# Four cross-attention layers on one core: wide layers' K and V projected in front of the layers, Q once per layer, one key tile for all queries per step

## The reference

```python
def _L0_xattn_ref(hidden_states, encoder_hidden_states, mask_A, mask_B, Wq, Wk, Wv, Wo, bo, ...):
    q, k, v = hidden_states @ Wq, encoder_hidden_states @ Wk, encoder_hidden_states @ Wv   # 16 heads of 64
    logits = jnp.einsum('bhqd,bhkd->bhqk', q, k) * scale + col_bias   # bias in two pairs of key columns
    probs = jax.nn.softmax(logits, axis=-1)
    out = jnp.einsum('bhqk,bhkd->bhqd', probs, v)
    return out.transpose(0, 2, 1, 3).reshape(B, HW, 1024) @ Wo + bo + residual
```

## Time and profile before

| | |
|---|---|
| median of 3 timed runs | 5464.57 us (5464.24 to 5474.47) |
| span of the profiled execution, first to last instruction | 5460.9 us |
| instructions | 81,559 |
| mean granted TensorE clock | 0.969 |
| DMA traffic | 116.57 MB |

### The profile page before, as it was taken

The page is one execution under the profiler, slowest core; times in us unless marked ns, Lnnn a source line. Parts: engine busy times, 40 slices in busy tenths (PEclk is TensorE's granted clock), DMA queues, the critical chain, the costliest instruction groups (busy, mean ns, idle before and its releaser), DMA issues.

```text
span 5460.9 us, 81559 instructions
## 1 busy us (share of the span) xinstructions
PE 5173.7 (95%) x21484; PEld 2708.9 (50%) x21484; DVE 3684.8 (67%) x5908; ACT 2245.5 (41%) x4042; POOL 2695.0 (49%) x2048
## 2 busy tenths in 40 slices
PE   7999999999979898987999999999989999999999
PEld 4455545554444444444455555555445455545554
DVE  6767676767667676765767666676676667676767
ACT  2433344334425455552444444344424444444443
POOL 1656565656510101011656566666625656565655
PEclk8999999999979999997999999999989999999999
DMA  2010101010020101001010101010011010101010
GB/s 72 14 27 14 27 14 27 14 27 14 14 43 15 24 16 23 16 15 26 14 26 13 26 13 26 13 26 19 8 28 24 16 26 13 26 13 26 13 26 17
DMA packets 40356, 116.57 MB, mean 21 GB/s; under 512 B 7350, under 2 KB 20150, under 8 KB 35068
## 3 DMA queue, kind: packets, MB, share of 16 engines
q1 hardware_dynamic: 39938, 112.04, 9.4%
HBM read 26.86 MB, written 2.10 MB: 5 GB/s over the span
## 4 chain that ended last, share of the span: by engine, by line
PE 82%; issue 7%; DVE 6%; DMA 2%; SPq 1%; ACT 0%; DVEq 0%; POOL 0%; ACTq 0%; POOLq 0%
PE OB L654 19%; PE SS L594 13%; PE ST L625 11%; PE ST L627 9%; PE ST L551 5%; PE ST L567 4%; PE OB L786 4%; DVE mpart L1087 4%; PE ST L765 3%; PE SS L744 3%; PE ST L572 3%; PE ST L672 3%; PE ZB L607 2%; DMA Q<-rawQ 1%; PE ZB L744 1%
## 5 line engine op out<-in xcount | busy, mean ns | idle before, releaser
L282 POOL TENSOR_TENSOR acc<-acc,P 128x512 f32<-128x512 f32 (+1 forms) x1776 | 2362.5, 1356 | 455.1 <-ACT P L934 308.8
L934 ACT ACTIVATE P<-ST 128x512 f32<-128x512 f32 (+1 forms) x2496 | 1385.5, 597 | 2012.0 <-PE ST L627 1703.7
L1087 DVE TENSOR_REDUCE mpart<-SS 128x1 f32<-128x400 f32 (+1 forms) x3072 | 1665.0, 563 | 764.1 <-PE SS L594 709.1
L654 PE MATMUL OB<-P,V 128*64 128x512 f32 (+1 forms) x4992 | 1348.0, 618 | 1.1
L594 PE MATMUL SS<-KS,Q 128*128 128x400 f32 (+1 forms) x3072 | 1171.6, 387 | 70.2 <-DVE mpart L1087 67.1
L625 PE MATMUL ST<-Q,K 128*128 128x512 f32 (+1 forms) x2496 | 1061.3, 425 | 32.9 <-issue 18.3
L594 PEld LDWEIGHTS SS<-KS,Q 128*128 128x128 f32 x3072 | 585.0, 192 | 860.0 <-DVE mpart L1087 758.5
L627 PE MATMUL ST<-Q,K 128*128 128x512 f32 (+1 forms) x2496 | 989.6, 396 | 0.0
L278 POOL TENSOR_TENSOR acc<-P 128x512 f32<-128x512 f32 x192 | 241.3, 1278 | 1410.8 <-ACT P L934 1310.8
L625 PEld LDWEIGHTS ST<-Q,K 128*128 128x128 f32 (+1 forms) x2496 | 462.8, 185 | 515.8 <-ACT P L934 348.3
L1106 DVE RECIPROCAL R<-ZB 128x64 f32<-128x64 f32 (+1 forms) x432 | 371.3, 860 | 408.9 <-PE ZB L607 408.9
(11 more groups left out here) (126 smaller groups left out, 3608.1 us busy)
## 6 DMA issues: line engine op xcount, KB each, us to landing
Q<-Q SPq DMA_DIRECT2D x48, 512.0 KB, 4.5
KS<-K SPq DMA_DIRECT2D x48, 400.5 KB, 3.8
K<-K SPq DMA_DIRECT2D x48, 400.5 KB, 5.3
Q<-Q SPq DMA_DIRECT2D x32, 256.0 KB, 4.3
wk<-in_wk SPq DMA_DIRECT2D x25, 256.0 KB, 4.4
wv<-in_wv SPq DMA_DIRECT2D x25, 256.0 KB, 4.6
Q<-rawQ SPq DMA_DIRECT2D x16, 256.0 KB, 3.8
wq<-in_wq SPq DMA_DIRECT2D x25, 128.0 KB, 4.3
```

The lines of the kernel that those rows point to most:

```text
L282: eng.tensor_tensor(out, out, P[0:rows_of(t), u % NP, :], ALU.add).then_inc(done, raised)
L654: last = pe.matmul(OB[64 * jj:64 * jj + 64, :], V[0:k, t, 64 * b:64 * b + 64], P[0:k, (2 * s + jj) % NP, :], start=t == 0, stop=t == KT - 1)
L934: act.activation(P[0:k, u % NP, :], ST[u % 4][0:k, :], ACT.Exp, scale=SCALE).then_inc(act_p, 1)
L1087: dve.tensor_reduce(mpart[:, i // len(KCH), i % len(KCH):i % len(KCH) + 1], SS[i % 2][:, 0:w], AX.X, ALU.max).then_inc(dve_s, 1)
```

## The change

The program has no hardware loops any more. In front of all layers, ctx is split into high and low parts (`ch`, `cl`), and so are the weights; K (all 24 pairs, and the narrow layer's K and V) and V (six quads of four pairs) are projected with three fp32r matmuls (high x high, high x low, low x high) per 128 channels instead of one in fp32, and go to tensors in HBM (`dK`, `dV`). The split Wq goes to `dWq`. At the start of a wide layer, `q_phase` projects Q of all heads in 32 items of 128 channels x 512 queries and stores both parts in `dQ`; from item 10 on the maxima tiles of the first head run between the items. A head's keys, queries and values are loaded by SP up to three heads ahead. A step of `head` is one key tile for four chunks of 512 queries, with three score banks `ST`, two value banks `OA`, `OB`, and three banks `SS` that maxima tiles, the transposed maxima, the sums and the output share in a fixed order (`RING`). `P` holds four key tiles of 2048. DVE adds the exponentials of key tiles 1 and 2, POOL those of 3 to 12, in halves of 1024. The output of a pair stands among the scores of the next pair's second head, at key tiles 0 to 3. The sums of a head come behind key tile 2 of the next. Maxima tiles run up to two heads ahead at key tiles 11 and 12. The narrow layer keeps its order, without loops, with its K and V from the front and 16 instead of 9 tiles of exponentials.

```diff
-NP = 6
-STEPS = 2 * KT
+NP = 4
+DVE_T = (1, 2)
+POOL_T = range(3, KT)
+NSTG = 6
+def s_tiles(h, t):
+    if t >= KT - 2:
+        return 2, (part(SUNITS, t - KT + 2, KT) if h + 2 < HEADS else range(0))
+    if h + 1 >= HEADS:
+        return 1, range(0)
+    return 1, (part(SUNITS, t, KT - 2) if h == 0 else part(SUNITS, t + 2, KT))
+def q_tiles(q):
+    first = 10
+    return part(SUNITS, q - first, QITEMS - first) if q >= first else range(0)
+def o_item(h, t, j):
+    if h % 2 == 1 and h >= 3 and t < 4 and j % 2 == 0:
+        return 2 * t + j // 2
+    return None
...
+            def project_k(m):
+                pe.wait_ge(dve_wk, m + 1)
+                for c, (o, w) in enumerate(KCH):
+                    at, b, k = BEFORE_AT["k", m, c], m % 2, slice(o, o + w)
+                    wait_bank(pe, at)
+                    bank = PB[at % 8][:, 0:w]
+                    for ct in range(CCT):
+                        pe.matmul(bank, wkh[b][:, ct, :], ch[:, ct, k], start=ct == 0, stop=False)
+                        pe.matmul(bank, wkh[b][:, ct, :], cl[:, ct, k], start=False, stop=False)
+                        last = pe.matmul(bank, wkl[b][:, ct, :], ch[:, ct, k], start=False, stop=ct == CCT - 1)
+                    last.then_inc(pe_k, 1)
...
+            def values(H, t):
+                k, e, n = rows_of(t), H % 2, H // 2
+                if t == 0:
+                    pe.wait_ge(d_v[n % 2], 16 * (n // 2 + 1))
+                    wait(pe, act_o, 2 * H)
+                pe.wait_ge(act_p, HU * H + JQ * t + JQ)
+                for j in range(JQ):
+                    r = 64 * (j % 2)
+                    last = pe.matmul(OAB[j // 2][r:r + 64, :], Vp[n % 2][0:k, t, 64 * e:64 * e + 64],
+                                     P[0:k, slot(H, t), j, :], start=t == 0, stop=t == KT - 1)
+                last.then_inc(pe_pv, 1)
...
+            def q_phase(l):
...
+                for q in range(QITEMS):
+                    n, p, j = QITEMS * l + q, q // JQ, slice(q % JQ * 512, q % JQ * 512 + 512)
...
+                    bank = ST[q % 3][:, :]
+                    for ct in range(CT):
+                        pe.matmul(bank, wqh[:, p, ct, :], xh[:, ct, j], start=ct == 0, stop=False)
+                        pe.matmul(bank, wqh[:, p, ct, :], xl[:, ct, j], start=False, stop=False)
+                        last = pe.matmul(bank, wql[:, p, ct, :], xh[:, ct, j], start=False, stop=ct == CT - 1)
+                    last.then_inc(pe_q, 1)
+                    for i in q_tiles(q):
+                        s_tile(H0, i)
...
+            def head(l, h):
+                H = l * HEADS + h
+                for t in range(KT):
+                    ahead, tiles = s_tiles(h, t)
+                    for j in range(JQ):
+                        if t + 1 < KT:
+                            scores(H, t + 1, j)
+                        elif h + 1 < HEADS:
+                            scores(H + 1, 0, j)
+                        if takes_row(h, t, j):
+                            transpose_max(H + 1)
+                        if o_item(h, t, j) is not None:
+                            output(l * PAIRS + (h - 3) // 2, o_item(h, t, j))
+                        for i in share(tiles, j):
+                            s_tile(H + ahead, i)
+                    values(H, t)
+                    if takes_sums(h, t):
+                        sums(H - 1)
...
+            def add(H, t):
+                for c in range(2):
+                    q = slice(2 * c, 2 * c + 2)
+                    out = acc[H % 2][:, q, :]
+                    dve.wait_ge(act_p, HU * H + JQ * t + 2 * c + 2)
+                    if t == 1:
+                        wait(dve, pe_z, 2 * (H - 1))
+                        dve.tensor_tensor(out, P[:, slot(H, 0), q, :], P[:, slot(H, 1), q, :], ALU.add).then_inc(dve_a, 1)
+                    else:
+                        dve.wait_ge(dve_a, 4 * H + c + 1)
+                        dve.tensor_tensor(out, out, P[:, slot(H, t), q, :], ALU.add).then_inc(dve_a, 1)
...
+                for t in range(KT):
...
+                    for j in range(JQ):
...
+                        for i in share(tiles, j):
+                            s_max(H + ahead, i)
+                    if t == KT - 3 and h + 1 < HEADS:
+                        head_max(H + 1)
+                    if t in DVE_T:
+                        add(H, t)
...
+                    if h > 0 and 3 <= t < 11:
+                        reciprocals(H - 1, t - 3)
+                    if h > 0 and t in (7, 8, 11, 12):
+                        divide(H - 1, (7, 8, 11, 12).index(t))
```

More of the change, by code:

```diff
@@ L50, with rows_of, words, part @@
 MROW = 3 * QD + D1
+NP = 4
+HU = KT * JQ
+QITEMS = PAIRS * JQ
+SROWS = D + 4
+MXROW = SROWS
+DVE_T = (1, 2)
+POOL_T = range(3, KT)
+NSTG = 6
+QUADS = BIG * PAIRS // 4
+NW = BIG * PAIRS + 2
 GUNITS = KT * JQ
 GSTEPS = range(0, KT - 2)
[L55 to L79, removed]
+def rows_of(t):
+    return KREST if t == KT - 1 else P128
+def words(ap):
+    return ap.bitcast(F32)
+def part(n, j, parts=4):
+    return range(n * j // parts, n * (j + 1) // parts)
+def s_tiles(h, t):
[4 more added lines that the diff above has]
+    return 1, (part(SUNITS, t, KT - 2) if h == 0 else part(SUNITS, t + 2, KT))
+def share(tiles, j):
+    return [tiles[i] for i in part(len(tiles), j)]
+def q_tiles(q):
[5 more added lines that the diff above has]
+    return None
+def takes_row(h, t, j):
+    return t == KT - 2 and j == 0 and h + 1 < HEADS
+def takes_sums(h, t):
+    return t == 2 and h > 0
 def g_s_units(t):
@@ L140, in attention_layers @@
[L140 to L156, removed]
@@ new lines, in attention_layers, with bank @@
+        dExt = dram("key_rows", (BIG, NROWS, KP))
+        dBias = dram("bias_rows", (2, 2, NQ))
+        def bank(name):
+            return ctx.enter_context(nc.psum_tensor(name, [128, 512], F32))
+        ST = [bank(f"ST{i}") for i in range(3)]
+        SS = [bank(f"SS{i}") for i in range(3)]
+        OA, OB = bank("OA"), bank("OB")
+        OAB = [OA, OB]
+        PB = ST + SS + [OA, OB]
+        GST = ST + [SS[2]]
+        GS = [SS[0], SS[1], OB]
+        GB = [SS[0], SS[1], OA, OB]
+        GOB, GZB = OA, OB
@@ L452, in _ @@
+            for l in range(BIG):
+                q_phase(l)
+                for h in range(HEADS):
+                    head(l, h)
+                if l == 0:
+                    group_layer()
             for t in range(0, QT, 4):
@@ new lines, in sums, with output @@
+            def sums(H):
+                pe.wait_ge(pool_a, 2 * len(POOL_T) * (H + 1))
+                for c in range(2):
+                    at = RING_AT["z", H, c]
+                    wait_ring(pe, at)
+                    for e in range(2):
+                        last = pe.matmul(SS[at % 3][64 * e:64 * e + 64, :], ones[:, 0:64], acc[H % 2][:, 2 * c + e, :],
+                                         start=True, stop=True)
+                    last.then_inc(pe_z, 1)
+            def output(n, i):
+                at, ct, j = RING_AT["o", n, i], i % CT, i // CT
+                if i == 0:
+                    pe.wait_ge(d_wo[n % 2], 16 * (n // 2 + 1))
+                if ct == 0:
+                    pe.wait_ge(dve_on, 4 * (2 * n + 1) + j + 1)
+                wait_ring(pe, at)
+                pe.matmul(SS[at % 3][:, :], wo[n % 2][:, ct * 128:(ct + 1) * 128], On[:, j * 512:(j + 1) * 512],
+                          start=True, stop=True).then_inc(pe_o, 1)
```

1746 lines of the change are left out of this document (894 added, 852 removed).

## The result

The changed kernel is slower: 6100.74 us median (6090.83 to 6108.97), against 5468.81 (5464.24 to 5474.47) for the kernel before on the same chip. The ratio is 1.1154, 95% interval 1.1139 to 1.117. The profiled execution has a span of 6089.0 us. The forecast was 5219 with a range of 5120 to 5440, so both the number and its sign were wrong.

A forecast was written before the change was run, and what follows sets the result against it. TensorE, busy 95% of the span, was taken to bound the kernel. Front 512, Q's phases 3 x 85 + 10, heads 3421, layer ends 66, narrow layer 941 and last stores 10 gave 5215, 5219 as median; range 5120 to 5440.

The forecast's parts named there:

- Q's phase: Start of each wide layer: 32 items of projection and stores, 85 us each of three times, bounds 70 and 120.
- rival (a): Transfers bind Q's phases: 117 us each at 234 GB/s, 5311 us in all; chance 0.13.
- (d): Slower rival: HBM stores far below all rows; 5451 us at 175 GB/s, some 5630 at 150; chance 0.05.
- The heads: Pairs of heads in wide layers: 144 us each, 141.7 counted plus stalls; 24 pairs 3456, less 35 gives 3421.
- the stall: Stalls within a pair of heads, taken as 2.3 us, bounds 0 and the 4.1 of before doubled.
- Rival (c): DVE's adds at key tiles 1 and 2 locked behind POOL, each waiting up to 2.5 us; 5493 us; chance 0.08.
- The front: Projections of K and V ahead of all layers: 512 us until Q's phase begins, stores hidden.
- (e): Rival: weight loads exposed, 0.19 us each, in the front and Q's phases add 524 us: 5739; chance 0.03.
- the switches (b): Rival: fp32r/fp32 changes not saved in the heads, 4.26 us a key tile, 125 us come back: 5340; chance 0.10.
- the narrow layer: Narrow layer: 953.5 us less its K and V projection and three loop returns, 941 us.
- idle before Q items, released by a store: Sign of being wrong: TensorE idle there in Q's phases would point to rivals (a) and (d).
- a mean clock under 0.95: Sign of being wrong: a mean clock below this value, named without a rival.

The follow-up runs named there:

- e4: Changed kernel with Q's high and low parts side by side in SBUF, one store per head ([64, 2, 512]); 5295.85 us, ratio 0.9694 to the kernel before.
- e8: e4 with POOL waiting before its adds of key tiles 8 and 9 for DVE's first and second division; 5080.0 us, ratio 0.9295 to the kernel before.
- e2: Changed kernel with the front's two per-head stores of a K part joined into one of [2, 64, 1602]; 6543.89 us, a single run.
- e6: e4 with key tile 3's add moved from POOL to DVE, divisions still on DVE; 5533.62 us, ratio 1.0124 to the kernel before.
- e7: e4 with POOL's adds in instructions of 512 columns instead of 1024, same work; 5510.1 us, ratio 1.0086 to the kernel before.

## Why the prediction was wrong, by its own steps

**Q's phase: the step that failed.** I costed its stores by a rate: between 234 and 335 GB/s, from the earlier trace rows. Those three rows are all of transfers with DMA shares of 0.56 to 1.06, none of them with an outermost axis of two. "16.8 MB of stores in 2 KB rows, a shape that the trace has as loads only" looked at the length of a row and not at the axis outside it, which stands in the diff (`dQ[p, :, 1, :, j]`, two heads outermost) and in the instruction's form. Measured were 51 GB/s, so neither rival (a) at 234 nor (d) at 175 or 150 reached far enough: the place and the sign of (d) were right, its cause was not, since it blamed HBM, and the DMA engines were 13% busy. The unknown was bounded by the nearest rows in size, and none of them had its form. 32 items x 10.28 are 329 of the 358.6 us; the row of maxima is queued on SP behind the last stores, and TensorE waits 58.3 for it.

With the stores repaired the step's own working holds: 88.6, 91.6 and 82 us in e4, 85 forecast. In e8 the first phase takes 88.1, from 520.2 to 608.3. That the K stores have their heads in a loop and Q's do not is the whole difference between a front on time (520.7, forecast 512) and phases four times too long; e2 shows it from the other side.

**The heads.** 147.4 a pair against 144 looks like a small miss, but two errors cancel in it. First, the base: 141.7 by counting, 138.0 in e8 where TensorE hardly stops. The term is the group of four values, which I took at twice 1.01 us = 2.02, and which is shorter:

```profile
1301.50 1.08 PE L767 MATMUL OA<-P,Vp 128*64 128x512 f32 x4
1302.41 1.03 PE L767 MATMUL OB<-P,Vp 128*64 128x512 f32 x4
1303.37 0.50 PE L755 MATMUL ST<-QX,KX 128*128 128x512 f32 x1
```

Start to start (e8) it is 1303.37 - 1301.50 = 1.87. I had read the 1.99 of the earlier trace rows as if it were a distance of starts, but a busy time runs on past the next start: the first row ends at 1302.58, the second begins at 1302.41. 26 x 0.15 = 3.9 against the 3.7 missing. Second, the stall: I took 2.3 a pair, and 9.4 were lost (147.4 less 138.0). 6.4 of them are the one wait; at 0.98 of the clock TensorE's own work also took 140.6 in place of 137.5. Behind it is a term of DVE's sum, "divisions 4 x 0.69": that is what a division takes alone, and here their mean is 2.22 us. That the total came near 144 is luck.

**Rival (c)** named the right pair of engines and the wrong instructions. I looked at DVE's adds at tiles 1 and 2, where POOL is idle, and put the wait behind POOL down as changing nothing there. DVE's divisions at tiles 7, 8, 11 and 12 read SBUF twice just as the adds do, and stand where POOL is busiest. My own count, 50 us of POOL's adds at the same pace as TensorE, said that POOL would have hardly a pause there. The price per case was wrong as well: I allowed one POOL instruction, 2.5 us, my estimate from the one add of 1.36 us in the earlier trace rows, and 8.45 were measured.

**What held.** The front (520.7 for 512), with projections of 400 columns 0.18 to 0.19 us apart, no further than one weight load of 0.19 takes, so weight loads are hidden and (e) falls; the switches (b), saved and more; the narrow layer, 943.6; the move of Q's projection out of the pairs. With the stores alone repaired the change takes 5295.85 (e4), inside the range and 77 above the forecast; with POOL's two waits, which the forecast did not have, it takes 5080.0, below the 5120 that bounded it. Of the signs named as wrong, "idle before Q items, released by a store" and "a mean clock under 0.95" both came true; the mean clock was 0.889.

**What stays open.** What exactly lets the division in. In e4, e6 and e7, too, the long ones end 0.54 to 0.55 us after POOL's last instruction before a pause, and in the changed kernel all 36 that met a pause of 0.14 to 0.81 us at the first end were let in. Without one, most got in between two adds and some did not, and nothing here tells the two apart. That the long ones end because TensorE's stall starves POOL is read from the order of the waits; no run tests it by itself. No run has the pause alone with the slow stores.

## What to carry to other kernels

Read the access pattern of every new DMA from the outside in before giving it a rate: here an outermost axis of 2 in place of 64 cost most of it (51 GB/s against 240 and 290, loads included). A low DMA share (0.13) beside a store that everyone waits for was the sign of it. Count the adds and divisions of DVE that take both inputs from SBUF and look for POOL's unbroken rows beside them; in the changed kernel DVE's other work did not stretch (reciprocals 0.89 to 0.96 us, maxima 0.55 to 0.58), while the divisions went from 0.66 to 8.61. Where POOL is nearly full, a wait put in on purpose at the right place was worth more than taking an add from it (a pair 8.9 us shorter in e8, 12.8 longer in e6, both against e4). A step that is bounded by neighbouring rows needs neighbours of the same form, not only of the same size.

## What the runs showed of the hardware that I had not expected

- A store of 256 KB with an outermost axis of two: 51 GB/s, 5.0 us each, DMA share 0.13, two packets under way at a time; the same bytes with 64 outermost 290 GB/s (loads included) at 0.91.
- A DVE division of 0.69 us beside an unbroken row of POOL adds mostly gets in at the end of one add (57 in the changed kernel), but some pass every end until POOL pauses: 8.45, 9.73, 10.39 and, in a layer's last head, 40.71 us, whether the adds last 1.30 or 2.43 us each.
- Taking an add away from POOL made a pair of heads 12.8 us longer (e6, 159.7 against 146.9 in e4); two added waits on POOL made it 8.9 us shorter (e8).
- TensorE at 28% busy ran at a granted clock of 0.50 (the changed kernel, 700 to 860 us). Its matmuls of 512 columns stood 0.427 us apart there, 1.2 columns per ns, which is the 1.2 GHz of the lower level, against 0.233 at a clock of 1.00. In e6's pairs, with two stalls of 7.7 us, the clock's mean fell to 0.94, where it was 1.00 in e8 without them.
